# Scores and exponentials of three heads at a time, in two sets of three PSUM banks

## The chip, the cores and the metric

The kernel runs on one core of a Trainium2 chip. The metric is the device time of one execution in microseconds (us). Before the change it is 911.02 us, the median of three runs (908.71 to 912.02).

## The reference

One block of a vision-language model: gated cross attention, then a gated feed-forward part. There are 4 batches of 512 rows of x with 512 channels, 1024 context rows per batch, 16 heads of 32 channels and 1536 hidden channels. Cut to what matters:

```python
q  = qdq(layernorm(x)) @ qdq(wq).T + bq              # qdq: fake int8 rounding
k, v = split(ctx @ wkv.T + bkv)
attn = softmax(einsum("bnhd,bmhd->bhnm", q, k) / sqrt(32))
o  = einsum("bhnm,bmhd->bnhd", attn, v)
x  = x + tanh(g_xattn) * (qdq(o) @ qdq(wp).T + bp)
y  = layernorm(x)
h  = silu((y @ gate_w) * gate_scale) * ((y @ up_w) * up_scale)
x  = x + tanh(g_ffn) * ((h @ down_w) * down_scale)
```

## The kernel before

The kernel is written engine by engine: each engine has its own program, in the order of the text, and semaphores tie them together. Batches are worked one after the other. For batch b TensorE (PE) runs the attention units, then a list `D_SEQ[b]` of products: the output projection, the next batch's keys, values and queries, the feed-forward part. Beside these, the next batch's row maxima are prepared (`maxima`, `differences`), from which comes a shift that each row of scores has subtracted, so that the exponential needs no maximum of its own.

**Units.** The attention of a batch has 4 groups (g) of 4 heads, and a group has 8 tiles (t) of 128 context rows: 32 units (u = 8 g + t). One unit is, for 4 heads j:

- `scores`: four f16 matmuls (97 rows deep, 128 keys by 512 queries), each into a PSUM bank of its own. L1569.
- the exponential on ScalarE (ACT), from PSUM into `prob` in SBUF (shown as tile r). L907. Before the change it takes two banks, so two heads, in one instruction of 128x1024.
- `values`: four f32 matmuls of 32 columns, side by side in TensorE, that add prob times the values into `O_BANK`. L1586. The trace shows each f32 matmul as two passes, so a unit as x8.
- the denominators: in batches 1 to 3, VectorE (DVE) adds up `prob` of the units t = 0 to 6 of a group in `acc` (`add_unit`, L1149, two adds of 128x1024 a unit, none at t = 0, whose prob goes in with t = 1). Then TensorE multiplies `acc` with a selector into `DEN_BANK` (`totals`, L1614, x8 in the trace). The last unit of a group, t = 7, isn't added by DVE but goes to TensorE itself (`sums`, L1600).

**Order on TensorE.** For each u: scores(u), values(u - 1), sums(u - 1) where that is a t = 7, and at t = 0 of a later group totals(g - 1). So the matmuls of the next unit's scores are queued behind totals, and totals waits for the last add of its group (`p_dve`).

**Buffers.** `prob` holds 12 heads, three units: the exponential of unit u waits until unit u - 3 has been used by `values` (`p_used`) and, if it is an added one, by DVE (`p_dve`). `acc` exists once: the first add of a group waits for the totals of the group before (`acc_read`), and that first add is what frees prob of the units t = 0 and t = 1. The output of a group is copied out of `O_BANK` by ACT (L911) before the next group's first `values` may start.

**PSUM banks in batches 1 to 3.** `SCORES[1] = (0, 6, 2)`: three pairs of banks, 0-1, 6-7 and 2-3, taken in turn, so the scores of pair n wait for the exponential of pair n - 3. Bank 4 is `O_BANK`, bank 5 `DEN_BANK`. While the stage before is still running, banks 4 to 7 serve the maxima (`DIFF`, `PAIR`) and 0 to 3 the products (`FREE_RING`).

**DVE** has one more job in the units of batches 1 and 2: the next batch's x (`x_ahead`: layer norm and rounding), a piece ahead of the add of each unit in `AHEAD_UNITS`, which is (3, 8 to 24). Batch 3 has none.

**DMA.** The stacked keys and queries (`kst`, `qst`) hold two groups. SyncE loads group g = 2 and 3 once the last scores of group g - 2 are issued: 24 DMAs and one for the shift row.

Batch 0 works in another way (single heads at first, no adds on DVE) and isn't touched by the change.

Of the kernel before, what the change touches and what calls it, by code (L numbers as in the profile page):

```python
# [8 lines left out]
ACT = mybir.ActivationFunctionType  # L9
# [6 lines left out]
P = 128  # L16
B, N, C = 4, 512, 512
M = 1024
H, DH = 16, 32
F = 1536  # L20
HG = P // DH
G = H // HG
# [13 lines left out]

FREE_RING, HEAD_RING = (0, 1, 2, 3), (0, 1, 2, 3, 4, 5)
O_BANK, DEN_BANK, PAIR = 4, 5, 6  # L40
DIFF, DIFF0 = 4, 2
SCORES = ((0, 2), (0, 6, 2))
K_SEQ0 = [f"K{n}" for n in (0, 2, 4, 6, 1, 3, 5, 7)]
TURNED = ["SX"] + [f"XT{c}" for c in range(CT)]
EARLY_V = ["V0", "V1"]
# [112 lines left out]
UNITS = G * MT  # L158
# [57 lines left out]
def v_out_count(name):  # L216
    return int(name[1:]) - len(EARLY_V) + 1
# [15 lines left out]
def d_seq(b):  # L233
    return D_SEQ[b]
# [11 lines left out]
def d_bank(b, name):  # L246
    return D_BANK[b][name]
# [33 lines left out]


def single(b, u):

    return b == 0 and u < SINGLES


def score_bank(b, u, j):
    if single(b, u):
        return j % 2  # L290
    return SCORES[b > 0][(2 * (u if b else u - SINGLES) + j // 2) % len(SCORES[b > 0])]


def diff_bank(b, s):
# [4 lines left out]
    return b * len(DIFFS) + DIFFS.index(s) + 1  # L299


def exp_count(b, u, j):

    if single(b, u):
        return HG * u + j + 1
    return HG // 2 * (b * UNITS + u + SINGLES) + j // 2 + 1


LAST_BANK = D_BANK[B - 1][f"DOWN{NT - 3}"]
# [21 lines left out]
def build(nc, ctxT, x, wq, wkvT, wp, gate_w, up_w, down_w, bqT, bkT, bv, bp, gsT, usT, ds,  # L331
          g_x, g_f, out):
    with ExitStack() as ctx:
# [452 lines left out]
        def _(act):  # L786
# [84 lines left out]
            def projection_weights(u):  # L871

                if u in WP_ROWS:
                    half = WP_ROWS.index(u)
                    integer_rows(DVE_WP, range(2 * half, 2 * half + 2))
                if ("W", 0, 0) in UNIT_MIDS0.get(u, []):
                    act.wait_ge(consts_in, 5 * 16)
                    act.wait_ge(act_setup, 1)
                    nc.scalar.activation(bp_bc[:, :], bp_bc[:, :], ACT.Copy, scale=tg_c[:, 0:1]).then_inc(act_setup, 1)
                    nc.scalar.activation(ds_bc[:, :], ds_bc[:, :], ACT.Copy, scale=tg_c[:, 1:2]).then_inc(act_setup, 1)  # L880
                    act.wait_ge(pe_setup, 2)
                    for half in range(2):
# [7 lines left out]
            act.wait_ge(pool_setup, 3)  # L890

            for b in range(B):
                nc.scalar.activation(table[:, :], zero[:, :], ACT.Exp)
                for u in range(UNITS):
                    g, t = divmod(u, MT)
                    freed = u - P_RING[b > 0]
                    if freed >= 0:
                        act.wait_ge(p_used, b * UNITS + freed + 1)
                    heads = 1 if single(b, u) else 2
                    for j in range(0, HG, heads):  # L900
                        if j == 2 and b == 0 and u >= 1:
                            differences(0, UNIT_STEPS0[u - 1])
                        if freed >= 0 and added(b, freed):
                            act.wait_ge(p_dve, add_count(b, freed, j + 1))
                        s, first_bank = p_slot(b, u, j), score_bank(b, u, j)
                        act.wait_ge(s_full, exp_count(b, u, j))
                        nc.scalar.activation(prob[:, s:s + heads, :], ps[:, first_bank:first_bank + heads, :], ACT.Exp,  # L907
                                             scale=SCALE).then_inc(exp_done, 1)
                    if t == 0 and g > 0:
                        act.wait_ge(o_full, b * G + g)  # L910
                        nc.scalar.copy(oT[:, g - 1, :], bank(O_BANK)).then_inc(o_out, 1)  # L911
                    if b == 0:
                        projection_weights(u)
                act.wait_ge(p_used, (b + 1) * UNITS)
                nc.scalar.copy(denT, bank(DEN_BANK)).then_inc(den_out, 1)  # L915
# [481 lines left out]
        def _(pe):  # L1397
# [147 lines left out]
            def scores(b, u, j):  # L1545

                g, t = divmod(u, MT)
                first_bank, n, ring = score_bank(b, u, j), 2 * u + j // 2, len(SCORES[b > 0])
                if t == 0 and j == 0:
                    rows = b if g % 2 else 0  # L1550
                    pe.wait_ge(stack_in[g % 2], ((b * 2 + g // 2 + 1) * STACK_DMAS + rows) * 16)
                if single(b, u):
                    if u == 0 and j < 2:
                        pe.wait_ge(v_out, v_out_count(f"V{MT - 1}"))
                    else:
                        pe.wait_ge(exp_done, exp_count(b, u, j) - 2)
                elif n >= (ring if b else 2 * SINGLES + ring):
                    pe.wait_ge(exp_done, exp_count(b, u, j) - ring)
                elif b == 0 and first_bank == DIFF0:
                    pe.wait_ge(diff_kept, len(DIFFS))  # L1560
                elif b == 0:
                    pe.wait_ge(exp_done, exp_count(b, u - 1, HG - 1))
                elif first_bank == PAIR:
                    pe.wait_ge(m_free, FREE_AFTER[b, STREAM[-1]])
                else:
                    for k in range(2):
                        released(b - 1, [n for n in d_seq(b - 1) if d_bank(b - 1, n) == first_bank + k][-1])
                for k in range(1 if single(b, u) else 2):
                    mm = nc.tensor.matmul(bank(first_bank + k), kst[0:97, g % 2, j + k, t * P:(t + 1) * P],  # L1569
                                          qst[0:97, g % 2, j + k, :], start=True, stop=True)  # L1570
                mm.then_inc(s_full, 1)

            def values(b, u):

# [19 lines left out]
            def sums(b, u):  # L1594

                if added(b, u):
                    return
                g = u // MT
                for j in range(HG):
                    mm = nc.tensor.matmul(ps[j * DH:(j + 1) * DH, DEN_BANK, :], esel[:, g, :],  # L1600
                                          prob[:, p_slot(b, u, j), :], start=(u == (MT - 1 if b else 0)), stop=(u == UNITS - 1))
                mm.then_inc(p_used, 1)

# [6 lines left out]
            def totals(b, g):  # L1610

                pe.wait_ge(p_dve, add_count(b, g * MT + ADDED[g][-1], HG - 1))
                for j in range(HG):
                    mm = nc.tensor.matmul(ps[j * DH:(j + 1) * DH, DEN_BANK, :], esel[:, g, :], acc[:, j, :],  # L1614
                                          start=False, stop=False)
                if g < G - 1:
                    mm.then_inc(acc_read, 1)
# [55 lines left out]

            for b in range(B):
                last = b == B - 1
                for u in range(UNITS):
                    g, t = divmod(u, MT)
                    scores(b, u, 0)
                    scores(b, u, 1 if single(b, u) else 2)
                    if u >= 1:  # L1680
                        values(b, u - 1)
                    if single(b, u):
                        scores(b, u, 2)
                        scores(b, u, 3)
                    for s in UNIT_MIDS0.get(u, []) if b == 0 else []:
                        maxima(b, s)
                    if u >= 1:
                        sums(b, u - 1)
                    for s in UNIT_STEPS0[u] if b == 0 else []:
                        maxima(b, s)  # L1690
                    if b > 0 and t == 0 and g > 0:
                        totals(b, g - 1)
                values(b, UNITS - 1)
                if b > 0:
                    totals(b, G - 1)
# [122 lines left out]
```

## Time and profile before

| what | us |
|---|---|
| median of three runs | 911.02 |
| the profiled execution | 908.2 |
| its span | 906.4 |
| TensorE busy | 852.7 (94%) |
| VectorE busy | 673.0 (74%) |
| ScalarE busy | 556.6 (61%) |
| attention units of batch 1, first exponential to the denominators' copy | 326.40 to 400.29 |
| the same of batch 2 | 538.68 to 612.84 |
| the same of batch 3 | 738.62 to 809.67 |

Busy times of TensorE come from pipelined matmuls whose ends are modelled: a share of 94% says that it is nearly always occupied, not that it works at its peak. The granted clock of TensorE was 0.998 of full speed over the span. In the rows, `ps` is PSUM, `r` the tile of prob, `vv` the values, `acc` the running sums, `qst` and `kst` the stacked queries and keys.

### The profile page before, as it was taken

Reading aid. Unit: us, or ns where it says so; the run is one execution under the profiler, and the core shown is the slowest. Engines: PE = TensorE matmul, PEld = TensorE weight load, DVE = VectorE, ACT = ScalarE, POOL = GpSimd, SP = SyncE. Lnnn points to the kernel's source line nnn. Section 1 sums busy time; section 2 is a strip of 40 time slices with the busy share of each in tenths; the row PEclk is TensorE's granted clock in tenths of the full one; section 3 lists DMA queues with packets and bytes.
Section 4 is the critical chain, followed back from the end, with each engine's and each line's share of the span. In section 5 each row is a group of like instructions: output and inputs, shape, how many; then the busy total and the mean of one; then the engine's idle time right before and its main releaser. Section 6 shows DMA issues by size and latency. Waiting matters only on the chain.

```text
span 906.4 us, 13628 instructions
## 1 busy us (share of the span) xinstructions
PE 852.7 (94%) x4974; PEld 314.0 (35%) x4982; DVE 673.0 (74%) x1300; ACT 556.6 (61%) x743; POOL 252.8 (28%) x241
## 2 busy tenths in 40 slices
PE   5989999999999999999899999999999989998998
PEld 1422222244333332234433332224433322234444
DVE  6877967989766788878666778986867778788222
ACT  5557988752466569772555659874356679862330
POOL 1335766872257400020017700002002210020230
PEclk9999999999999999999999999999999999999999
DMA  9334244221211332100111143200010023200001
GB/s 329 105 97 125 84 118 116 80 83 49 50 36 47 99 106 62 44 1 1 44 33 48 38 117 101 67 1 1 15 39 1 1 63 102 53 1 24 12 0 47
DMA packets 37251, 55.29 MB, mean 61 GB/s; under 512 B 8960, under 2 KB 15424, under 8 KB 37184
## 3 DMA queue, kind: packets, MB, share of 16 engines
q1 hardware_dynamic: 35264, 48.13, 18.7%
q0 software_dynamic: 1920, 6.29, 2.3%
q8 instruction: 39, 0.64, 0.3%
q14 instruction: 28, 0.23, 0.1%
HBM read 31.21 MB, written 4.19 MB: 39 GB/s over the span
## 4 chain that ended last, share of the span: by engine, by line
PE 69%; DVE 15%; ACT 8%; issue 7%; DMA 1%; ACTq 0%; DVEq 0%
PE ps L1418 34%; PE ps L1606 9%; PE ps L1586 8%; PE ps L1569 8%; ACT r L907 5%; PE ps L1541 4%; DVE acc L1149 4%; PE ps L1600 4%; PE ps L1614 1%; DVE kst L1124 1%; DVE am L1004 1%; PE ps L1402 1%; DVE xs L1334 1%; DVE r L1290 1%; ACT r L930 1%
## 5 line engine op out<-in xcount | busy, mean ns | idle before, releaser
L907 ACT ACTIVATE r<-ps 128x1024 f32<-128x1024 f32 (+1 forms) x300 | 253.3, 902 | 53.6 <-PE ps L1569 51.1
L1124 DVE CUSTOM_DVE_ANT_0 kst<-ps,kst 128x512 f32<-128x512 f32 x192 | 124.5, 685 | 30.3 <-PE ps L1541 28.9
L1586 PE MATMUL ps<-r,vv 128*32 128x512 f32 x1024 | 137.3, 608 | 3.4 <-ACT r L907 3.2
L1569 PE MATMUL ps<-qst,kst 97*128 97x512 f16 x512 | 138.0, 384 | 2.6 <-ACT r L907 1.4
L1149 DVE TENSOR_TENSOR acc<-acc,r 128x1024 f32<-128x1024 f32 x120 | 138.6, 1215 | 0.0
L861 ACT ACTIVATE kst<-ps 128x1024 f32<-128x1024 f32 x96 | 98.1, 1022 | 54.2 <-PE ps L1474 53.9
L1418 PE MATMUL ps<-xs,w_gate 128*128 128x512 f16 x384 | 91.0, 380 | 2.0 <-DVE xs L1334 2.0
L1418 PE MATMUL ps<-xs,w_up 128*128 128x512 f16 x384 | 91.1, 380 | 0.0
L1569 PEld LDWEIGHTS ps<-qst,kst 97*128 97x128 f16 x512 | 40.5, 97 | 139.3 <-ACT r L907 88.1
L962 ACT ACTIVATE qst<-ps,gs_c 128x512 f32<-128x512 f32 x48 | 33.0, 687 | 68.0 <-PE ps L1418 68.0
L1364 DVE SCALAR_TENSOR_TENSOR xq<-ps,us_c,qst 128x512 f32<-128x512 f32 x48 | 36.0, 749 | 50.6 <-PE ps L1418 50.6
L1606 PE MATMUL ps<-w_down,r 128*128 128x512 f16 (+1 forms) x312 | 66.2, 363 | 0.0
L1418 PE MATMUL ps<-ctx_hi,wkv_hi 128*128 128x512 f16 x128 | 49.1, 389 | 14.3 <-ACT ctx_hi L797 10.9
L777 POOL TENSOR_TENSOR r<-xq,r 128x512 f16<-128x512 f32 x36 | 42.6, 1183 | 70.4 <-ACT r L955 70.0
L1474 PE MATMUL ps<-acc,q_reg 32*128 32x512 f16 x256 | 49.7, 384 | 4.7 <-issue 3.6
L1541 PE MATMUL ps<-k_reg,q_reg 32*128 32x512 f16 x256 | 49.7, 385 | 4.5 <-DVE mx L1124 3.9
L1418 PEld LDWEIGHTS ps<-xs,w_gate 128*128 128x128 f16 x384 | 35.6, 98 | 47.0 <-issue 5.2
L727 POOL TENSOR_TENSOR xres<-xres,bp_bc 128x512 f32<-128x512 f32 x12 | 14.9, 1269 | 129.7 <-ACT r L915 129.1
L1418 PEld LDWEIGHTS ps<-xs,w_up 128*128 128x128 f16 x384 | 34.6, 98 | 45.0 <-issue 8.1
L688 POOL TENSOR_TENSOR rstd<-mv,mhalf 128x4 f32<-128x4 f32 x8 | 9.9, 1240 | 141.4 <-DVE mv L1035 141.4
L1418 PE MATMUL ps<-ctx_lo,wkv_hi 128*128 128x512 f16 x128 | 48.9, 387 | 0.3 <-DVE ctx_lo L1159 0.3
L1149 DVE TENSOR_TENSOR acc<-r 128x1024 f32<-128x1024 f32 x24 | 28.3, 1222 | 27.7 <-ACT r L907 27.7
(173 smaller groups left out, 1347.9 us busy)
## 6 DMA issues: line engine op xcount, KB each, us to landing
kst<-k_reg SPq DMA_DIRECT2D x192, 64.0 KB
qst<-q_reg SPq DMA_DIRECT2D x192, 32.0 KB
xs<-in_x SPq DMA_DIRECT2D x4, 1024.0 KB, 5.9
cf<-in_ctxT POOLq DMA_DIRECT2D x16, 256.0 KB, 3.4
xres<-in_x SPq DMA_DIRECT2D x3, 1024.0 KB, 5.2
out<-xres SPq DMA_DIRECT2D x12, 256.0 KB, 2.0
acc<-in_down_w SPq DMA_DIRECT2D x10, 256.0 KB, 2.6
vv<-in_wkvT SPq DMA_DIRECT2D x2, 1024.0 KB, 9.7
```

Source lines behind the costliest of these rows:

```text
L777: nc.gpsimd.tensor_tensor(f2_at(b, 1, i), fus[:, i % 2, :], f2_at(b, 0, i), ALU.subtract).then_inc(f_ready, 1)
L861: nc.scalar.activation(kept(b, n), ps[:, first_bank:first_bank + 2, :], ACT.Relu, scale=2.0).then_inc(diff_kept, 1)
L907: nc.scalar.activation(prob[:, s:s + heads, :], ps[:, first_bank:first_bank + heads, :], ACT.Exp, scale=SCALE).then_inc(exp_done, 1)
L1124: ins = nc.vector.tensor_tensor_reduce(kept(b, n)[:, k, :], bank(PAIR + k), kept(b, n)[:, k, :], 1.0, -3.0e38, ALU.add, ALU.max, mx[:, g % ...
L1149: nc.vector.tensor_tensor(sums, other, prob[:, p:p + ADD_HEADS, :], ALU.add).then_inc(p_dve, 1)
L1418: mm = nc.tensor.matmul(out, l, r, start=(k == 0), stop=(k == len(terms) - 1))
L1474: mm = nc.tensor.matmul(bank(first_bank + k), qhi[rows, g, i // 2 * P:(i // 2 + 1) * P], kdiff[rows, g % 2, :], start=True, stop=True)
L1541: mm = nc.tensor.matmul(bank(PAIR + k), qhi[rows, g, t * P:(t + 1) * P], khi[rows, g, 512:1024], start=True, stop=True)
L1569: mm = nc.tensor.matmul(bank(first_bank + k), kst[0:97, g % 2, j + k, t * P:(t + 1) * P], qst[0:97, g % 2, j + k, :], start=True, stop=True)
L1586: mm = nc.tensor.matmul(ps[j * DH:(j + 1) * DH, O_BANK, :], vv[:, t, h * DH:(h + 1) * DH], prob[:, p_slot(b, u, j), :], start=(t == 0), st ...
L1600: mm = nc.tensor.matmul(ps[j * DH:(j + 1) * DH, DEN_BANK, :], esel[:, g, :], prob[:, p_slot(b, u, j), :], start=(u == (MT - 1 if b else 0) ...
L1606: mm = nc.tensor.matmul(out[:, cols], f2_at(b, part, i)[:, t * P:(t + 1) * P], w_down[:, i, cols], start=(i == 0 and part == 0), stop=(i = ...
```

## The change

In batches 1 to 3 the 128 heads of a batch's units are no longer handled in 64 pairs but in 43 steps of three (the last has two). A step may hold heads of two units. `THREES = (5, 0)`: steps take banks 5, 6, 7 and banks 0, 1, 2 in turn, so step n waits for the exponential of step n - 2. The denominators move from bank 5 to bank 3 in these batches. TensorE issues the scores of step n, and then values and sums of each unit whose last head lies in a step up to n - 2; totals(g - 1) now stands behind values of the next group's first unit, and no longer ahead of it.

```diff
-O_BANK, DEN_BANK, PAIR = 4, 5, 6
+O_BANK, DEN_BANK, PAIR = 4, (5, 3), 6
-SCORES = ((0, 2), (0, 6, 2))
+SCORES, THREES = (0, 2), (5, 0)
...
+def three(n):
+
+    return range(3 * n, min(3 * n + 3, UNITS * HG))
...
+STEPS_0 = HG * SINGLES + HG // 2 * (UNITS - SINGLES)
+STEPS_B = -(-UNITS * HG // 3)
...
+                for n in range(STEPS_B if b > 0 else 0):
+                    heads = three(n)
+                    freed = sorted({h // HG - P_RING[1] for h in heads})
+                    if freed[-1] >= 0:
+                        act.wait_ge(p_used, b * UNITS + freed[-1] + 1)
+                    for u in freed:
+                        if u >= 0 and added(b, u):
+                            act.wait_ge(p_dve, add_count(b, u, heads[-1] % HG if u == freed[-1] else HG - 1))
+                    s, first_bank = p_slot(b, 0, heads[0]), THREES[n % 2]
+                    act.wait_ge(s_full, exp_count(b, 0, heads[0]))
+                    nc.scalar.activation(prob[:, s:s + len(heads), :], ps[:, first_bank:first_bank + len(heads), :],
+                                         ACT.Exp, scale=SCALE).then_inc(exp_done, 1)
+                    for h in heads:
+                        g, first = divmod(h - HG + 1, MT * HG)
+                        if first == 0 and g > 0:
+                            turned_out(b, g)
...
+            def scores_of_three(b, n):
+                first_bank = THREES[n % 2]
+                for h in three(n):
+                    if h % (MT * HG) == 0:
+                        stacked(b, h // (MT * HG))
+                if n >= 2:
+                    pe.wait_ge(exp_done, STEPS_0 + (b - 1) * STEPS_B + n - 1)
+                elif first_bank == DIFF + 1:
+                    pe.wait_ge(diff_kept, (b + 1) * len(DIFFS))
+                    pe.wait_ge(m_free, FREE_AFTER[b, STREAM[-1]])
+                else:
+                    for k in range(3):
+                        products_done(b, first_bank + k)
+                for k, h in enumerate(three(n)):
+                    mm = score(b, h // HG, h % HG, first_bank + k)
+                mm.then_inc(s_full, 1)
...
-                    if b > 0 and t == 0 and g > 0:
-                        totals(b, g - 1)
+                done = UNITS - 1 if b == 0 else 0
+                for n in range(STEPS_B + 2 if b > 0 else 0):
+                    if n < STEPS_B:
+                        scores_of_three(b, n)
+                    while done < UNITS - 1 and (done * HG + HG - 1) // 3 <= n - 2:
+                        values(b, done)
+                        sums(b, done)
+                        if done % MT == 0 and done > 0:
+                            totals(b, done // MT - 1)
+                        done += 1
```

The start of batch 1's units on TensorE, before. L1606 is the last product of the stage ahead (bank 3), L1569 are scores, L1586 values:

```order
L1606 MATMUL ps<-w_down,r 128x512 x8
L1569 MATMUL ps<-qst,kst 128x512 x8
L1586 MATMUL ps<-r,vv 32x512 x4
L1569 MATMUL ps<-qst,kst 128x512 x4
L1586 MATMUL ps<-r,vv 32x512 x4
L1569 MATMUL ps<-qst,kst 128x512 x4
```

The same place after the change, where L1659 are the products, L1583 scores and L1637 values:

```order
L1659 MATMUL ps<-w_down,r 128x512 x8
L1583 MATMUL ps<-qst,kst 128x512 x12
L1637 MATMUL ps<-r,vv 32x512 x4
L1583 MATMUL ps<-qst,kst 128x512 x3
L1637 MATMUL ps<-r,vv 32x512 x4
L1583 MATMUL ps<-qst,kst 128x512 x3
L1637 MATMUL ps<-r,vv 32x512 x4
L1583 MATMUL ps<-qst,kst 128x512 x6
```

Twelve heads of scores now stand ahead of the first values, not eight. From there on, blocks of 3, 3 and 6 score matmuls alternate with values, where there were blocks of 4; the number of blocks is one for each unit either way.

The first border between groups on TensorE, from values(6) on, before. L1600 are sums, L1614 totals:

```order
L1586 MATMUL ps<-r,vv 32x512 x4
L1569 MATMUL ps<-qst,kst 128x512 x4
L1586 MATMUL ps<-r,vv 32x512 x4
L1600 MATMUL ps<-r,esel 32x512 x4
L1614 MATMUL ps<-acc,esel 32x512 x4
L1569 MATMUL ps<-qst,kst 128x512 x4
L1586 MATMUL ps<-r,vv 32x512 x4
L1569 MATMUL ps<-qst,kst 128x512 x4
```

The same after the change, with L1653 sums and L1667 totals:

```order
L1637 MATMUL ps<-r,vv 32x512 x4
L1583 MATMUL ps<-qst,kst 128x512 x3
L1637 MATMUL ps<-r,vv 32x512 x4
L1653 MATMUL ps<-r,esel 32x512 x4
L1583 MATMUL ps<-qst,kst 128x512 x3
L1637 MATMUL ps<-r,vv 32x512 x4
L1667 MATMUL ps<-acc,esel 32x512 x4
L1583 MATMUL ps<-qst,kst 128x512 x6
L1637 MATMUL ps<-r,vv 32x512 x4
L1583 MATMUL ps<-qst,kst 128x512 x3
```

Between sums and totals there are now three score matmuls and the values of unit 8. Behind totals come six score matmuls and values(9).

## Rows read from the trace of the kernel before

**Rows 1.** Windows inside batch 1's units, no border inside: us, then busy (x) of PE, PEld, DVE, ACT.
```profile
331.50:341.30 9.80, 9.80 (x64) 2.30 (x62) 9.77 (x16) 9.58 (x11) 1.89 (x1) 1.00 0.42 137
346.90:358.70 11.80, 11.80 (x76) 2.80 (x72) 11.80 (x13) 11.64 (x13) 0.00 (x0) 1.00 0.33 77
```
**Rows 2.** Chain of waits in batch 1's units: start, length, engine, tile, line.
```profile
326.40 1.95 ACT r L907 x2
...
330.52 0.99 PE ps L1586 x8
331.52 0.97 PE ps L1569 x4
...
342.31 1.00 PE ps L1586 x8
343.31 0.86 PE ps L1600 x8
344.17 0.86 PE ps L1614 x8
345.68 1.03 ACT r L907
...
396.12 1.03 ACT r L907
397.19 1.07 PE ps L1586 x8
398.29 1.07 PE ps L1614 x8
```
**Rows 3.** ScalarE in order of time: batch 1 behind its three borders, batch 3 behind one.
```profile
345.68 15.72 ACT L907 ACTIVATE r<-ps 128x1024 f32<-128x1024 f32 x16 [1.27 <-PE ps L1569]
...
364.99 15.70 ACT L907 ACTIVATE r<-ps 128x1024 f32<-128x1024 f32 x16 [3.11 <-PE ps L1569]
...
383.40 13.73 ACT L907 ACTIVATE r<-ps 128x1024 f32<-128x1024 f32 x14 [2.24 <-PE ps L1569]
...
757.90 15.70 ACT L907 ACTIVATE r<-ps 128x1024 f32<-128x1024 f32 x16 [1.27 <-PE ps L1569]
```
**Rows 4.** ScalarE's groups by shape, whole span: busy, mean ns, idle before.
```profile
L907 ACT ACTIVATE r<-ps 128x1024 f32<-128x1024 f32 x212 | 205.0, 1023 | 44.6 <-PE ps L1569 42.1
...
L907 ACT ACTIVATE r<-ps 128x512 f32<-128x512 f32 x88 | 48.3, 610 | 9.0 <-PE ps L1569 9.0
```
**Rows 5.** Order of time on TensorE, batch 1: start of the units, and values(15).
```profile
320.57 3.19 PE L1606 MATMUL ps<-w_down,r 128*128 128x512 f16 x14
...
325.77 2.32 PE L1569 MATMUL ps<-qst,kst 97*128 97x512 f16 x8
...
327.48 0.11 PEld L1569 LDWEIGHTS ps<-qst,kst 97*128 97x128 f16 x2 [0.57 <-ACT r L907]
...
328.49 1.06 PE L1586 MATMUL ps<-r,vv 128*32 128x512 f32 x8 [0.40 <-ACT r L907]
...
359.69 1.07 PE L1586 MATMUL ps<-r,vv 128*32 128x512 f32 x8
```
**Rows 6.** The same, start of batch 3's units.
```profile
736.79 0.38 PE L1606 MATMUL ps<-w_down,wkv_hi 128*128 128x512 f16 x1
738.00 1.46 PE L1569 MATMUL ps<-qst,kst 97*128 97x512 f16 x6 [0.83 <-issue]
```
**Rows 7.** Order of time on VectorE, in batch 1's second group.
```profile
346.81 1.23 DVE L1149 TENSOR_TENSOR acc<-r 128x1024 f32<-128x1024 f32 x1 [2.29 <-ACT r L907]
...
358.00 2.35 DVE L1149 TENSOR_TENSOR acc<-acc,r 128x1024 f32<-128x1024 f32 x2
```
**Rows 8.** TensorE's waits in batch 1's units: total, times, longest.
```profile
PE ps L1614 <- DVE acc L1149: 2.4, 2, 1.7
```
**Rows 9.** SyncE's queue in batch 3's units, in order of time.
```profile
770.04 7.52 SPq L555 DMA_DIRECT2D qst<-q_reg  x12
777.61 7.80 SPq L555 DMA_DIRECT2D kst<-k_reg  x12
785.45 0.63 SPq L565 DMA_DIRECT2D qst<-crow  x1
```

More of the change, by code:

```diff
@@ L285, in single, with score_bank @@
     return b == 0 and u < SINGLES
[L288 to L291, printed above, removed]
+def score_bank(u, j):
+    return j % 2 if single(0, u) else SCORES[(2 * (u - SINGLES) + j // 2) % 2]
+def three(n):
+    return range(3 * n, min(3 * n + 3, UNITS * HG))
 def diff_bank(b, s):
@@ L299, in diff_count @@
     return b * len(DIFFS) + DIFFS.index(s) + 1
+STEPS_0 = HG * SINGLES + HG // 2 * (UNITS - SINGLES)
+STEPS_B = -(-UNITS * HG // 3)
 def exp_count(b, u, j):
+    if b > 0:
+        return STEPS_0 + (b - 1) * STEPS_B + (u * HG + j) // 3 + 1
     if single(b, u):
         return HG * u + j + 1
-    return HG // 2 * (b * UNITS + u + SINGLES) + j // 2 + 1
+    return HG // 2 * (u + SINGLES) + j // 2 + 1
 LAST_BANK = D_BANK[B - 1][f"DOWN{NT - 3}"]
@@ L890, in _, with turned_out @@
             act.wait_ge(pool_setup, 3)
+            def turned_out(b, g):
+                if added(b, g * MT - 1):
+                    act.wait_ge(p_used, b * UNITS + g * MT)
+                else:
+                    act.wait_ge(o_full, b * G + g)
+                nc.scalar.copy(oT[:, g - 1, :], bank(O_BANK)).then_inc(o_out, 1)
             for b in range(B):
                 nc.scalar.activation(table[:, :], zero[:, :], ACT.Exp)
-                for u in range(UNITS):
+                for u in range(UNITS if b == 0 else 0):
                     g, t = divmod(u, MT)
-                    freed = u - P_RING[b > 0]
+                    freed = u - P_RING[0]
                     if freed >= 0:
-                        act.wait_ge(p_used, b * UNITS + freed + 1)
+                        act.wait_ge(p_used, freed + 1)
                     heads = 1 if single(b, u) else 2
                     for j in range(0, HG, heads):
-                        if j == 2 and b == 0 and u >= 1:
+                        if j == 2 and u >= 1:
                             differences(0, UNIT_STEPS0[u - 1])
-                        if freed >= 0 and added(b, freed):
-                            act.wait_ge(p_dve, add_count(b, freed, j + 1))
-                        s, first_bank = p_slot(b, u, j), score_bank(b, u, j)
+                        s, first_bank = p_slot(b, u, j), score_bank(u, j)
                         act.wait_ge(s_full, exp_count(b, u, j))
@@ L909, in _ @@
                     if t == 0 and g > 0:
[L910 to L913, printed above, removed]
+                        turned_out(b, g)
+                    projection_weights(u)
+                for n in range(STEPS_B if b > 0 else 0):
[13 more added lines that the diff above has]
+                        if first == 0 and g > 0:
+                            turned_out(b, g)
                 act.wait_ge(p_used, (b + 1) * UNITS)
-                nc.scalar.copy(denT, bank(DEN_BANK)).then_inc(den_out, 1)
+                nc.scalar.copy(denT, bank(DEN_BANK[b > 0])).then_inc(den_out, 1)
                 nc.scalar.copy(oT[:, G - 1, :], bank(O_BANK)).then_inc(o_out, 1)
@@ L1543, in maxima, with stacked, score @@
                 mm.then_inc(m_full, 1)
-            def scores(b, u, j):
+            def stacked(b, g):
+                rows = b if g % 2 else 0
+                pe.wait_ge(stack_in[g % 2], ((b * 2 + g // 2 + 1) * STACK_DMAS + rows) * 16)
+            def score(b, u, j, out):
                 g, t = divmod(u, MT)
[L1548 to L1559, printed above, removed]
-                    pe.wait_ge(diff_kept, len(DIFFS))
-                elif b == 0:
-                    pe.wait_ge(exp_done, exp_count(b, u - 1, HG - 1))
-                elif first_bank == PAIR:
@@ new lines, in score, with scores @@
+                return nc.tensor.matmul(bank(out), kst[0:97, g % 2, j, t * P:(t + 1) * P], qst[0:97, g % 2, j, :],
+                                        start=True, stop=True)
+            def scores(u, j):
+                first_bank = score_bank(u, j)
+                if u % MT == 0 and j == 0:
+                    stacked(0, u // MT)
+                if u == 0 and j < 2:
+                    pe.wait_ge(v_out, v_out_count(f"V{MT - 1}"))
+                elif single(0, u) or u > SINGLES:
+                    pe.wait_ge(exp_done, exp_count(0, u, j) - 2)
+                elif first_bank == DIFF0:
+                    pe.wait_ge(diff_kept, len(DIFFS))
+                else:
+                    pe.wait_ge(exp_done, exp_count(0, u - 1, HG - 1))
+                for k in range(1 if single(0, u) else 2):
+                    mm = score(0, u, j + k, first_bank + k)
+                mm.then_inc(s_full, 1)
@@ L1565, in scores @@
                 else:
[L1566 to L1570, printed above, removed]
+                    for k in range(3):
+                        products_done(b, first_bank + k)
@@ L1571, in scores, with products_done @@
+                for k, h in enumerate(three(n)):
+                    mm = score(b, h // HG, h % HG, first_bank + k)
                 mm.then_inc(s_full, 1)
+            def products_done(b, bank_no):
+                released(b - 1, [n for n in d_seq(b - 1) if d_bank(b - 1, n) == bank_no][-1])
             def values(b, u):
@@ L1597, in sums @@
                     return
+                if b > 0 and u == MT - 1:
+                    products_done(b, DEN_BANK[1])
                 g = u // MT
                 for j in range(HG):
-                    mm = nc.tensor.matmul(ps[j * DH:(j + 1) * DH, DEN_BANK, :], esel[:, g, :],
+                    mm = nc.tensor.matmul(ps[j * DH:(j + 1) * DH, DEN_BANK[b > 0], :], esel[:, g, :],
                                           prob[:, p_slot(b, u, j), :], start=(u == (MT - 1 if b else 0)), stop=(u == UNITS - 1))
@@ L1613, in totals @@
                 for j in range(HG):
-                    mm = nc.tensor.matmul(ps[j * DH:(j + 1) * DH, DEN_BANK, :], esel[:, g, :], acc[:, j, :],
+                    mm = nc.tensor.matmul(ps[j * DH:(j + 1) * DH, DEN_BANK[b > 0], :], esel[:, g, :], acc[:, j, :],
                                           start=False, stop=False)
@@ L1675, in _ @@
                 last = b == B - 1
[L1676 to L1679, printed above, removed]
+                for u in range(UNITS if b == 0 else 0):
+                    scores(u, 0)
+                    scores(u, 1 if single(b, u) else 2)
                     if u >= 1:
@@ L1682, in _ @@
                     if single(b, u):
-                        scores(b, u, 2)
-                        scores(b, u, 3)
-                    for s in UNIT_MIDS0.get(u, []) if b == 0 else []:
+                        scores(u, 2)
+                        scores(u, 3)
+                    for s in UNIT_MIDS0.get(u, []):
                         maxima(b, s)
@@ L1688, in _ @@
                         sums(b, u - 1)
-                    for s in UNIT_STEPS0[u] if b == 0 else []:
+                    for s in UNIT_STEPS0[u]:
                         maxima(b, s)
-                    if b > 0 and t == 0 and g > 0:
-                        totals(b, g - 1)
+                done = UNITS - 1 if b == 0 else 0
[8 more added lines that the diff above has]
+                        done += 1
+                assert done == UNITS - 1
                 values(b, UNITS - 1)
```

## The prediction, made blind

> **What bounds the units now.** I read first the windows of each stage, then the chain of waits inside the attention units, then ScalarE and VectorE in order of time there, and last the waits by engine. Only the units of batches 1 to 3 change, some 70 us each, so nothing outside them is priced.
>
> Within a group TensorE is busy 9.80 of 9.80 us and 11.80 of 11.80 [rows 1]. ScalarE looks full too (11.64 of 11.80), but its rows carry the write-back, which overlaps with the next instruction: two exponentials take 1.95 us and one 1.03, so a new one can start every 0.92 us, 1.84 us a unit [rows 2]. Sixteen of them, eight units, in fact took 15.72 us, 1.96 us a unit [rows 3]. That is TensorE's pace: the chain goes through nothing but scores (0.97) and values (0.99), 1.96 us [rows 2]. ScalarE has about 0.12 us of slack a unit.
>
> At a border between groups 0.86 for sums and 0.86 for totals come in, and ScalarE then idles 1.27 us behind its copy of the output [rows 2, 3]. This is TensorE's work, and stays. Behind the second and third border of batch 1 it idles 3.11 and 2.24 us instead [rows 3]: 1.84 + 0.97 = 2.8 us more, because totals waits for VectorE's last add (2.4 us in two waits [rows 8]). Batch 2 has these two again, batch 3, without next x on VectorE, none.
>
> **Exponentials of three.** 64 instructions a batch become 43. From 610 ns for 512 columns and 1023 for 1024 [rows 4] I take 413 to 430 ns a bank, so 1.45 us for 1536, and a new one every 0.92 + 0.43 = 1.35 us. This is the unknown operation; its bounds are 1.38 (two banks and a quarter less for the third) and 1.63 (the two rows added). ScalarE's need falls from 1.84 to 1.80 us a unit. TensorE's stays: four score matmuls, one block of values and two changes of kind a unit, 1.96 us. So the steady stretch gains nothing. It may lose a little: with two sets of banks, where two steps of scores stand together, the second needs an exponential that has just ended. A score matmul takes (3.19 - 0.38)/13 = 0.216 us [rows 5, 6], so a block of three takes 0.97 - 0.22 = 0.75 with the change of kind, 0.65 without. If a step's scores start at 0, its exponential starts at 0.85 and ends at 2.30; the scores two steps on are due at 0.75 + 0.99 + 0.65 = 2.39. That is nearly free: 0 to 0.05 us for each such pair, 0.2 us a batch.
>
> The Trainium skill (Perfetto Trace Analysis, "Optimizing Scalar/DVE Operations") says that larger ScalarE operations raise throughput if that engine is saturated, with some 51 ns of overhead for each one on PSUM. By the rule, an estimate, the 21 instructions saved would give 1.1 us a batch. The same section says that where ScalarE is not saturated but causes gaps on others, smaller instructions can be better; the trace puts this kernel on that side.
>
> **The start, per batch +0.9.** Before, from the first score matmul to values(0) it is 328.49 - 325.77 = 2.72 us, 8 score matmuls inside [rows 5]. After: first exponential at 0.85 (0.63 now and a third matmul), end 2.30, scores of step 2 at 2.36 (0.06 after an exponential's end, as at 327.48 [rows 2, 5]); second exponential at 0.85 + 1.35 = 2.20, end 3.65, scores of step 3 at 3.71, values(0) at 4.46. Four more matmuls are inside, 0.86 us of work done early. Loss: 4.46 - 2.72 - 0.86 = 0.9.
>
> In batch 3 the first scores wait 0.83 us and more for bank 0, which VectorE still empties [rows 6]. After, step 0 takes banks 5 to 7 and can follow the last product at 736.79 + 0.22: 1.0 us earlier. So -1.0 in batch 3. In batches 1 and 2 bank 3 held the last product, and its wait is already in the 2.72.
>
> **The borders: the ring of prob behind late totals.** This is the step I put most weight on. acc is single: totals(g - 1), then the first add of group g, then prob of that group's unit 0 is free, then the exponential three units on may start. Totals now stands one unit later, but the ring is still three units. For the first border, from the start of totals: totals 1.07 [rows 2], 0.10 to VectorE (an exponential ended at 346.71, the add began at 346.81 [rows 2, 7]), the first half of the add 1.23 [rows 7], 0.10 to ScalarE, the exponential of step 14 1.45, 0.05 to TensorE: scores of step 16 at 4.00. TensorE's own work until there: totals with change of kind 0.99, six score matmuls with a change 1.40, values 0.99: 3.38. It idles 0.6. At the second border the same count comes out, 0.6. At the third the step that needs the ring holds three heads of one unit, so both halves of the add are needed (+1.13): 5.1 against 0.99 + 0.75 + 0.99 + 0.75 + 0.99 = 4.5, a wait of 0.65, and the next step follows without values between (0.65 against ScalarE's 1.35): 0.7 more. Sum of a batch: 0.6 + 0.6 + 1.35 = 2.6 us. In batch 3 this is all new.
>
> In batches 1 and 2 totals no longer waits for the add, -2.8 us. But VectorE paces the second group: its adds and pieces of x follow one another without a gap. Its first add starts later than now. From the start of values(7) the order gives values 0.89, sums 0.97, scores 0.75, values(8) 0.89, totals 1.07 and 0.10, so 4.67; now it is 346.81 - 342.31 = 4.50 [rows 2, 7]. And values(7) itself comes 1.6 us later, 0.9 from the start and 0.65 for three heads more that are issued ahead of it. So +1.75. The half of unit 13's add that the exponential of head 64 needs ends at 358.00 + 1.22 now, then at 360.97; exponential from 361.07 to 362.52, scores of step 23 at 362.6. TensorE is at this point of its work, where values(15) is the next block of values, at 359.69 now [rows 5]; with one score matmul more (0.2) and the 1.55 lost so far (0.9, 0.6 and a steady pair) it is there at 361.45. Wait 1.1. Behind it I expect smaller ones of this kind, 0.7 together (bounds 0 and 1.5). So the wait on VectorE isn't removed but moves from totals into the ring. Borders of batch 1: 2.6 + 1.1 + 0.7 - 2.8 = +1.6, and batch 2 alike.
>
> **The end of the units.** Before, TensorE waits 0.76 us for the last exponential and 0.2 for the last add (397.19 after values(30), 398.29 [rows 2]). After, the last step has two heads and starts sooner, but the last add then decides: 0.9 in sum. 0, bounds -0.4 and +0.5. The denominators in bank 3: 0, since that bank's last product is long out at unit 7.
>
> **Sum.** Batch 1: 0.9 + 0.2 + 1.6 = 2.7; batch 2: 2.7; batch 3: 0.9 + 0.2 + 2.6 - 1.0 = 2.7. Together +8.1 on the profiled 908.2, so 916.3. The median is 2.8 above the profiled run, so 919.0 us. No change can be told below 0.5%, 4.6 us.
>
> **Rivals.**
> - *No stall from the ring.* If VectorE's first add of a group starts soon enough, or the exponentials run further behind than I count, the 2.6 us a batch and the 1.1 + 0.7 fall away. Batches 1 and 2: 0.9 + 0.2 - 2.8 = -1.7 each, batch 3 +0.1: 907.7 us. For it: VectorE idles 2.29 us at the first border now [rows 7]. Against: that gap ends with an exponential behind totals, and the order puts totals still later. A case between, with half the stalls, is 913.5.
> - *ScalarE is what paces.* Then what it saves counts: 64 x 0.92 - 43 x 1.35 = 0.8 us a batch, or 21 x 0.16 = 3.4 if an instruction's whole fixed part falls away (610 less 430 to 450 ns for the columns), besides the 2.8 of two batches: 911 - 5.6 - 2.4 to 10.2, so 895 to 903. Against: 1.96 is TensorE's sum to the hundredth. By the skill's 51 ns this would be 3.2 us over three batches beside the 5.6.
> - *Slower still, by the keys' DMA.* Group 3's loads take 785.45 + 0.63 - 770.04 = 16.0 us to issue, from the last scores of group 1 [rows 9]. TensorE needs them 8 units of 1.96 and a border of 1.7 and a little later, 18.1 now. After the change a step reaches over a group's border and values are issued further behind, so the need comes at 17.4. If the last load takes over 1.4 us to land, each of up to 6 borders waits up to 1 us: 922 to 925.
> - *A dearer exponential.* At 1.55 us the start, the borders and the steady pairs each grow by one or two tenths: +2.3 in all, 921.3. At 1.63, 923.
>
> **Chances.** My sum with small deviations (916 to 921) 0.55; with the DMA or a dearer exponential (above 921) 0.17; half the stalls (911 to 916) 0.13; no stall 0.09; ScalarE as the pace 0.06. Range 911.5 to 923.5, which leaves the last two and the far end out. Faster by over 0.5% (below 906.5) 0.06, within 0.5% 0.18, slower by over 0.5% (above 915.6) 0.76.
>
> **What would show it.** Right: in the changed profile each exponential of 128x1536 near 1.45 us; inside groups TensorE still 1.96 us a unit; no wait of totals on VectorE before the last; instead scores waiting for exponentials behind each border, and ScalarE idle there until an add ends; values(0) some 4.5 us behind the first score matmul, where it is 2.7 now. Wrong: exponentials that start without a wait for an add three units back; ScalarE without gaps and units of 1.80 us; or a wait on stack DMAs of a microsecond at the borders.

## The result and the profile after

| | median us | against the kernel before |
|---|---|---|
| before | 910.5 (6 runs) | |
| after | 918.2 (916.3 to 920.0, 6 runs) | ratio 1.008, 95% interval 1.0061 to 1.0098 |

The change makes the kernel slower, by 7.7 us. The forecast was 919.0, between 911.5 and 923.5. The profiled execution of after has a span of 914.4 us, 8.0 more than before.

The page of after shows first what the change was able to do. Section 1, busy time and instructions of each engine:

```profile
PE 856.9 (94%) x4982; PEld 312.2 (34%) x4982; DVE 673.7 (74%) x1300; ACT 550.8 (60%) x680; POOL 253.1 (28%) x241
```

ScalarE has 63 instructions fewer and 5.8 us less busy time. Its exponentials of three, in the stretch of batch 1's units, by shape (out and in, count, busy us, mean ns, idle before and what ended it; batch 1's last step, of two heads, isn't among them):

```profile
L939 ACT ACTIVATE r<-ps 128x1536 f32<-128x1536 f32 x42 | 59.1, 1454 | 17.5 <-PE ps L1583 10.7 <-DVE acc L1180 6.4
```

1454 ns is the 1.45 us of the prediction. Before, all the idle time ahead of batch 1's exponentials was ended by score matmuls. Now 6.4 us of it is ended by an add of VectorE.

The start of batch 1's units on TensorE, in order of time, answers to [rows 5]:

```profile
326.08 1.46 PE L1583 MATMUL ps<-qst,kst 97*128 97x512 f16 x6
328.43 0.82 PE L1583 MATMUL ps<-qst,kst 97*128 97x512 f16 x3 [0.90 <-ACT r L939]
329.77 0.82 PE L1583 MATMUL ps<-qst,kst 97*128 97x512 f16 x3 [0.52 <-ACT r L939]
330.52 1.07 PE L1637 MATMUL ps<-r,vv 128*32 128x512 f32 x8
```

Values(0) starts 4.44 us after the first score matmul; it was 2.72. The third and fourth steps each wait for an exponential.

The chain of waits in batch 1 answers to [rows 2], first inside the first group, then from values(7) over the border:

```profile
337.54 0.75 PE ps L1583 x3
338.29 0.99 PE ps L1637 x8
339.29 0.76 PE ps L1583 x3
340.04 0.99 PE ps L1637 x8
341.04 1.45 PE ps L1583 x6
342.49 0.99 PE ps L1637 x8
...
344.24 0.99 PE ps L1637 x8
345.24 0.86 PE ps L1653 x8
346.10 0.75 PE ps L1583 x3
346.85 1.00 PE ps L1637 x8
347.85 0.90 PE ps L1667 x8
348.77 1.28 DVE acc L1180 x2
```

Three units now take 0.75 + 0.99 + 0.76 + 0.99 + 1.45 + 0.99 = 5.93 us of TensorE; before they took 3 x 1.96 = 5.88. A third head in one instruction bought nothing in the steady stretch, as it is TensorE's. What is new is that the chain leaves TensorE behind totals and goes on through VectorE. The same border in order of time, all engines:

```profile
348.77 2.36 DVE L1180 TENSOR_TENSOR acc<-r 128x1024 f32<-128x1024 f32 x2 [3.47 <-PE ps L1667]
...
350.08 4.14 ACT L939 ACTIVATE r<-ps 128x1536 f32<-128x1536 f32 x3 [1.49 <-DVE acc L1180]
...
351.59 0.82 PE L1583 MATMUL ps<-qst,kst 97*128 97x512 f16 x3 [0.49 <-ACT r L939]
```

VectorE is idle for 3.47 us until totals has read `acc`, ScalarE for 1.49 us until the first add has freed prob, TensorE for 0.49 until that exponential is done. In [rows 7] VectorE's idle time at this place was 2.29 us and ended by an exponential.

For the whole stretch, from the start of the last product ahead of the units to the copy of the denominators (us, from the rows of each profile; before in batch 1: 325.55 to 400.29):

| profile | batch 1 | batch 2 | batch 3 | sum | against before |
|---|---|---|---|---|---|
| before | 74.7 | 75.0 | 72.9 | 222.6 | |
| after | 77.2 | 77.2 | 76.0 | 230.4 | +7.7 |
| threes_totals_early | 76.6 | 75.0 | 74.7 | 226.2 | +3.6 |
| threes_early_pool_keys | 75.0 | 75.0 | 73.6 | 223.5 | +0.9 |
| pairs_totals_late | 72.3 | 72.3 | 73.4 | 218.0 | -4.6 |
| pairs_late_bank6 | 72.3 | 72.3 | 72.2 | 216.8 | -5.8 |
| pairs_late_two_sets | 75.6 | 75.6 | 75.7 | 226.9 | +4.2 |
| pairs_short_exp | 74.2 | 74.5 | 72.7 | 221.4 | -1.2 |

The 7.7 us of the change are these stretches; all that lies outside them is 0.3 us longer than before.

### The profile page after: what moved, and what is told of

It reads as the page before. It is cut to its first block, busy times and chain, and to the rows that moved or that the text cites. A ratio compares the mean times of both kernels' runs of the same rounds, so it can differ in the third digit from the quotient of the medians.

```text
span 914.4 us, 13570 instructions
## 1 busy us (share of the span) xinstructions
PE 856.9 (94%) x4982; PEld 312.2 (34%) x4982; DVE 673.7 (74%) x1300; ACT 550.8 (60%) x680; POOL 253.1 (28%) x241
## 4 chain that ended last, share of the span: by engine, by line
PE 67%; DVE 16%; ACT 8%; issue 7%; SPq 2%; DMA 1%; ACTq 0%; DVEq 0%
PE ps L1449 33%; PE ps L1659 9%; PE ps L1583 7%; PE ps L1637 7%; DVE acc L1180 5%; PE ps L1572 4%; ACT r L939 4%; PE ps L1653 4%; SPq L566 2%; PE ps L1667 1%; DVE kst L1155 1%; ACT r L924 1%; PE ps L1433 1%; DVE am L1035 1%; DVE xs L1365 1%
## 5 line engine op out<-in xcount | busy, mean ns | idle before, releaser
L939 ACT ACTIVATE r<-ps 128x1536 f32<-128x1536 f32 (+1 forms) x129 | 180.0, 1444 | 47.4 <-PE ps L1583 29.2
L1583 PE MATMUL ps<-qst,kst 97*128 97x512 f16 x512 | 141.0, 385 | 14.7 <-ACT r L939 12.4
L1637 PE MATMUL ps<-r,vv 128*32 128x512 f32 x1024 | 137.2, 608 | 0.6
L872 ACT ACTIVATE kst<-ps 128x1024 f32<-128x1024 f32 x96 | 98.2, 1023 | 54.2 <-PE ps L1505 53.9
L1583 PEld LDWEIGHTS ps<-qst,kst 97*128 97x128 f16 x512 | 38.5, 97 | 156.8 <-ACT r L939 75.6
L924 ACT ACTIVATE r<-ps 128x512 f32<-128x512 f32 (+1 forms) x108 | 67.7, 686 | 18.3 <-PE ps L1583 18.3
L1659 PE MATMUL ps<-w_down,r 128*128 128x512 f16 (+1 forms) x312 | 66.2, 363 | 0.0
```

What stands on the lines that cost most here:

```text
L872: nc.scalar.activation(kept(b, n), ps[:, first_bank:first_bank + 2, :], ACT.Relu, scale=2.0).then_inc(diff_kept, 1)
L939: nc.scalar.activation(prob[:, s:s + len(heads), :], ps[:, first_bank:first_bank + len(heads), :], ACT.Exp, scale=SCALE).then_inc(exp_done, 1)
L1583: return nc.tensor.matmul(bank(out), kst[0:97, g % 2, j, t * P:(t + 1) * P], qst[0:97, g % 2, j, :], start=True, stop=True)
L1637: mm = nc.tensor.matmul(ps[j * DH:(j + 1) * DH, O_BANK, :], vv[:, t, h * DH:(h + 1) * DH], prob[:, p_slot(b, u, j), :], start=(t == 0), st ...
L1659: mm = nc.tensor.matmul(out[:, cols], f2_at(b, part, i)[:, t * P:(t + 1) * P], w_down[:, i, cols], start=(i == 0 and part == 0), stop=(i = ...
```

## Experiments

Each run was timed beside fresh executions of the kernel before, and its ratio is against those: their median was 910.9 us for the first four runs below, and 911.2 for the last two. The clock of TensorE isn't the same in all executions, and two medians can differ by it; the last section and the account ahead of it say by how much.

**threes_totals_early** takes the late totals out of the changed kernel and leaves the steps of three:

```diff
-                        if done % MT == 0 and done > 0:
-                            totals(b, done // MT - 1)
+                        if done % MT == MT - 1:
+                            totals(b, done // MT)
```

> The changed kernel, but totals of a group stand right behind sums of its last unit, ahead of the next score matmuls, as in the kernel before. Theory (late totals hold the ring of prob: first add late, so the exponential three units on late): the waits of scores behind the borders (0.5 at the first, up to 1.4 with ScalarE behind it) go at the first and third border; the wait of totals on VectorE comes back in part in batches 1 and 2 (about 0.5 us at the third border). About 2.1 us less in each of the three batches, so 918.2 - 6.4 = 911.8 us, near the kernel before (within 0.3%). Rival (the loss comes from the three-head steps themselves, totals' place is harmless or useful): at least as slow as the changed kernel, 918 to 922 us, since VectorE's waits of 2.8 us in two batches come back.

Measured: 914.2 us (12 runs), ratio 1.0032 (1.0017 to 1.0047) against 1.008. So late totals costs 4.0 us by the medians of the two kernels, and the rival, that it is harmless, falls. ScalarE at the same border, in order of time:

```profile
347.22 1.46 ACT L939 ACTIVATE r<-ps 128x1536 f32<-128x1536 f32 x1
349.26 1.45 ACT L939 ACTIVATE r<-ps 128x1536 f32<-128x1536 f32 x1 [0.58 <-PE ps L1583]
351.01 1.45 ACT L939 ACTIVATE r<-ps 128x1536 f32<-128x1536 f32 x1 [0.30 <-PE ps L1583]
```

No exponential waits for an add there now. But the time is 2.4 us above what I expected. By stretches: batch 1 has a spell at a lower granted clock (last section), 1.6 us of this profile; without it, batches 1 and 2 lie 0.3 and 0.0 above the kernel before, as expected, and batch 3 lies 1.8 above, where 2.1 us less than the changed kernel would be 1.1. TensorE waits for the shift row's DMA, the last load of a group, longer than in the changed kernel. Batch 2 has two such waits and batch 3 one of 0.5 us; the last line is a second one of batch 3, seen from the weight load, while the matmul's own row puts its 0.82 us on an exponential:

```profile
573.39 0.82 PE L1583 MATMUL ps<-qst,kst 97*128 97x512 f16 x3 [0.60 <-DMA qst<-crow]
...
592.09 0.82 PE L1583 MATMUL ps<-qst,kst 97*128 97x512 f16 x3 [0.47 <-DMA qst<-crow]
...
772.53 0.33 PEld L1583 LDWEIGHTS ps<-qst,kst 97*128 97x128 f16 x3 [1.72 <-DMA qst<-crow]
```

**pairs_totals_late** is the other corner: the kernel before, with late totals only.

```diff
-                    if b > 0 and t == 0 and g > 0:
+                    if b > 0 and t == 1 and g > 0:
                         totals(b, g - 1)
```

> The kernel before with its pairs and three sets of two banks, but totals of a group one unit later. Theory (the ring has room for late totals as long as pairs are issued less far ahead, and VectorE's wait at the borders was the only recoverable loss): TensorE's waits for VectorE in batches 1 and 2 nearly vanish, 2.3 us each, batch 3 loses 0.3 us at most: 910.5 - 4.3 = 906.2 us. Rival (late totals stall the ring here as they do with threes): the 2.8 us saved at the borders come back as waits of scores for exponentials, and batch 3 loses 1 to 2 us: 910.5 to 913 us.

Measured: 906.6 us (8 runs), ratio 0.9943 (0.9922 to 0.9965). Against the 910.9 beside it, the same move that costs 4 us with the threes gains 4.3 with the pairs. TensorE's waits in batch 1's units, where [rows 8] had 2.4 us on VectorE:

```profile
PE ps L1614 <- DVE acc L1149: 0.3, 1, 0.3
```

ScalarE in order of time shows why the ring doesn't stall it:

```profile
361.92 0.58 ACT L911 COPY k_reg<-ps 128x512 f32<-128x512 f32 x1
362.77 2.11 ACT L907 ACTIVATE r<-ps 128x1024 f32<-128x1024 f32 x2 [0.28 <-DVE acc L1149]
365.58 9.82 ACT L907 ACTIVATE r<-ps 128x1024 f32<-128x1024 f32 x10 [0.70 <-PE ps L1569]
```

Once it is held for 0.28 us by an add, in a place where it has that slack. The stretches of batches 1 and 2 fall from 74.7 and 75.0 to 72.3 us, by 2.4 and 2.7 where 2.3 each was expected. Batch 3 grows from 72.9 to 73.4, by 0.6 where at most 0.3 was expected; a score matmul there waits 0.2 us for the shift row's DMA.

**pairs_late_bank6** also changes the order of the pairs' sets: `SCORES = ((0, 2), (6, 0, 2))`, where the last entry was (0, 6, 2).

> As the one before, with the pairs' sets in the order 6, 0, 2 instead of 0, 6, 2: the first pair of a batch no longer takes the bank that the last product still holds in batch 3. Theory: first scores of batch 3 start 0.9 to 1.0 us earlier (before 1.2 us behind the last product's last matmul), nothing changes in batches 1 and 2: 905.2 us. Rival (the start there waits for the maxima or the keys' DMA): no difference from the one before, 906.2 us.

Measured: 904.9 us (6 runs), ratio 0.9931 (0.9906 to 0.9955); this is the lowest median of all. The times don't separate it from the one before, the trace does: batch 3's stretch is 72.2 and not 73.4. Its start answers to [rows 6]:

```profile
733.02 0.38 PE L1606 MATMUL ps<-w_down,wkv_hi 128*128 128x512 f16 x1
733.24 0.60 PE L1569 MATMUL ps<-qst,kst 97*128 97x512 f16 x2
734.19 1.47 PE L1569 MATMUL ps<-qst,kst 97*128 97x512 f16 x6 [0.35 <-DVE acc L1224]
```

The first scores follow the product after 0.22 us, where there were 1.21.

**pairs_short_exp** asks whether ScalarE paces the units. It leaves work out: in batches 1 to 3 an exponential covers 448 of 512 columns.

```diff
-                        nc.scalar.activation(prob[:, s:s + heads, :], ps[:, first_bank:first_bank + heads, :], ACT.Exp,
-                                             scale=SCALE).then_inc(exp_done, 1)
+                        cols = N if b == 0 else N - 64
+                        nc.scalar.activation(prob[:, s:s + heads, 0:cols], ps[:, first_bank:first_bank + heads, 0:cols],
+                                             ACT.Exp, scale=SCALE).then_inc(exp_done, 1)
```

> The kernel before, but in batches 1 to 3 each exponential covers 448 of the 512 columns of its two heads (the others keep what prob held), so each is about 0.11 us shorter. Theory (TensorE paces the units, ScalarE has slack): units stay at 1.96 us; only starts and ends of a batch gain, 0.3 to 0.5 us each: 909.3 us, within the noise. Rival (ScalarE paces, and saving there would count): 64 x 0.11 = 6.8 us a batch, about 890 us.

Measured: 910.3 us (10 runs), ratio 0.9993 (0.9978 to 1.0008). Each exponential fell from 1023 to 916 ns, and its start to start could too, but in order of time two of them are followed by a gap, every 1.96 us:

```profile
336.23 1.73 ACT L908 ACTIVATE r<-ps 128x896 f32<-128x896 f32 x2 [0.24 <-PE ps L1570]
338.19 1.73 ACT L908 ACTIVATE r<-ps 128x896 f32<-128x896 f32 x2 [0.24 <-PE ps L1570]
340.16 1.73 ACT L908 ACTIVATE r<-ps 128x896 f32<-128x896 f32 x2 [0.24 <-PE ps L1570]
```

The rival, about 890 us, falls: the units keep TensorE's period. What is taken off ScalarE turns into ScalarE's idle time, so what only makes the exponentials cheaper is worth 0.2 to 0.5 us a batch here, at the ends.

**pairs_late_two_sets** takes a set away from the pairs: `SCORES = ((0, 2), (6, 0))`, all else as in pairs_totals_late.

> As pairs_totals_late, but with two sets of two banks (6-7 and 0-1) instead of three, so the scores of pair n wait for the exponential of pair n - 2. Theory (two sets are part of the price of the threes: TensorE can no longer run ahead of ScalarE over its values block): scores wait for exponentials inside groups too, values(0) comes later, about 3.2 us more in each batch than pairs_totals_late, less the 1.0 us that batch 3 gains at its start: 906.5 + 8.6 = 915.1 us. Rival (a third set is never needed in the steady stretch, only late totals cost): 905.5 to 907.5 us.

Measured: 914.3 us (10 runs), ratio 1.0038 (1.0022 to 1.0054). So 7.7 us for the third set; the stretches say 8.9, and I had expected 8.6. In order of time ScalarE now loses 0.27 us after every fourth exponential, inside the group:

```profile
334.72 3.99 ACT L907 ACTIVATE r<-ps 128x1024 f32<-128x1024 f32 x4 [0.40 <-PE ps L1569]
338.97 3.98 ACT L907 ACTIVATE r<-ps 128x1024 f32<-128x1024 f32 x4 [0.27 <-PE ps L1569]
```

So the third set is what the pairs live on. The ring of prob isn't what it guards: with two sets of pairs TensorE's waits in batch 1 are 1.0 and 0.4 us, at the start and at the end, and none stands behind a border. That points to the steps of three and their order of issue for the stall behind late totals, and not to the missing set alone; it isn't proof, as two units of pairs take 4.25 us here and not 3.92, which gives the ring some time. The changed kernel has late totals and two sets too, and its stretches take 230.4 us where this one's take 226.9: with late totals, steps of three heads don't repay the third set, they add 3.5 us to its loss. Whether they would with early totals wasn't tried.

**threes_early_pool_keys** takes threes_totals_early and lets GpSimd issue the key loads of groups 2 and 3, beside SyncE's loads of the queries and with semaphores of their own (TensorE's waits for them are left out here):

```diff
-                    stack(kst, (khi, khi, klo), g, upto[3:])
                     if b == 0:
+                        stack(kst, (khi, khi, klo), g, upto[3:])
...
+                    for g in range(2, G):
+                        pool.wait_ge(s_full, exp_count(b, (g - 1) * MT - 1, HG - 1))
+                        for dst4, src in enumerate((khi, khi, klo)):
+                            for j in range(HG):
+                                pool.dma_start(kst[dst4 * DH:(dst4 + 1) * DH, g % 2, j, :],
+                                               src[j * DH:(j + 1) * DH, g, :]).then_inc(keys_in[g % 2], 16)
```

> As threes_totals_early, but in batches 1 to 3 the twelve key DMAs of groups 2 and 3 are issued by GpSimd, beside SyncE's twelve of the queries, so that the last load of a group is issued some 7 us sooner. Theory (the 1.1 us that threes_totals_early lies above its expectation is score matmuls that wait for the last of a group's DMAs): the waits on the shift row's DMA (1.1 us in batch 2, 0.5 in batch 3) vanish: about 1.6 us less, 912.6 us. Rival (GpSimd's descriptors slow VectorE's adds, or the keys come later still from that queue): waits on VectorE or on the keys grow, 914 to 920 us.

Measured: 914.4 us (10 runs), ratio 1.0023 (1.0009 to 1.0037), where 912.6 us was expected. The interval overlaps that of threes_totals_early, so the time alone is inconclusive. In the trace the waits on the DMA are gone in all three batches. Batch 3 gains 1.1 us, and its 0.82 us of above is gone too, so that was the DMA. Batch 2 gains nothing: there VectorE's adds and its pieces of x pace the units. The 1.1 us of DMA wait in batch 2 are replaced: TensorE's waits on ScalarE grow from 1.7 to 2.6 us and those on VectorE from 0.5 to 0.7, 3.3 in sum with either kernel:

```profile
PE ps L1593 <- ACT r L946: 2.6, 4, 0.9
PE ps L1677 <- DVE acc L1187: 0.7, 2, 0.5
```

## Why the prediction was right, point by point

- *TensorE bounds the units.* Shown: after the change the chain keeps to TensorE inside batch 1's first group, and shorter exponentials change nothing in the kernel before. In the second group of batch 1 the chain runs through VectorE's adds, as the prediction had it.
- *An exponential of three banks takes 1.45 us and a new one starts every 1.35.* 1454 ns measured, and two in a row take 2.80 us, so 1.35 from start to start. Right.
- *Steady stretch 0 to 0.05 us a pair of steps that stand together.* 5.93 against 5.88 us for three units. Right.
- *Start: values(0) at 4.46.* 4.44. The loss of 0.9 us a batch stands. The removed third set is its cause only in part: pairs_late_two_sets, with eight heads ahead of it as before, has values(0) at 3.2, 0.5 later than before.
- *Batch 3 starts 1.0 us earlier.* Its first scores follow the last product in 0.22 us, before 1.21. Right.
- *The ring behind late totals.* Right at all three borders; the links (totals to VectorE, first half of the add, exponential, scores) stand in the rows in that order, and taking totals back removes the stalls. The idle time in a row counts from the modelled end of the matmul ahead, and the prediction counted from the time at which the block was due, so the two can't be set side by side. Counted in the prediction's way: at the first border values start at 350.03 and take 1.00, so scores were due at 351.03 and start at 351.59, 0.56 late, against 0.6. At the second it is 0.55 against 0.6, at the third 0.59 and 0.69 against 0.65 and 0.7. That is 2.4 us in a batch, against 2.6. The second and the third border of batch 1:

```profile
371.27 0.82 PE L1583 MATMUL ps<-qst,kst 97*128 97x512 f16 x3 [0.38 <-ACT r L939]
...
391.21 0.82 PE L1583 MATMUL ps<-qst,kst 97*128 97x512 f16 x3 [0.52 <-ACT r L939]
392.55 0.82 PE L1583 MATMUL ps<-qst,kst 97*128 97x512 f16 x3 [0.52 <-ACT r L939]
```

- *VectorE's pace in group 1.* I put 1.1 us on the scores of step 23 at 362.6. They start at 362.85; they were due 0.65 behind 361.04, so 1.16 late. Behind it I had 0.7 in smaller waits, and scores are 0.26 late at 365.72, 0.42 at 379.39 and 0.12 at 384.5, 0.8 together:

```profile
362.85 0.82 PE L1583 MATMUL ps<-qst,kst 97*128 97x512 f16 x3 [0.99 <-ACT r L939]
...
365.72 0.82 PE L1583 MATMUL ps<-qst,kst 97*128 97x512 f16 x3 [0.19 <-ACT r L939]
```

- *End of the units: 0.* Counted in the same way, the blocks at the end of batch 1 are 0.16, 0.20 and 0.54 late, 0.9 together, where they were 0.85 and 0.22, 1.1 together: -0.2, within the bounds. As predicted, the last add now decides.
- *Sum.* I had 2.7 us for each batch. Measured are 2.4, 2.1 and 3.2 in the stretches, 7.7 against 8.1. The terms of batch 1 as measured are start 0.86, ring 2.39, VectorE 1.16 and 0.80, less 2.79 of totals' waits (1.84 and 0.95 late before) and less 0.2 at the end: 2.2, which leaves 0.2 for the steady stretches, as I had it. That the total comes within 0.4 us is in part luck, as the batches miss to both sides. The third is larger because of a rival that I had given a small chance, the keys' DMA: in batch 3 the weight load of the first score step of group 2 waits for the last DMA of the group (the idle time of the weight queue, of which 0.84 stands before any such block):

```profile
775.52 0.33 PEld L1583 LDWEIGHTS ps<-qst,kst 97*128 97x128 f16 x3 [1.29 <-DMA qst<-crow]
794.18 0.34 PEld L1583 LDWEIGHTS ps<-qst,kst 97*128 97x128 f16 x3 [1.18 <-DMA qst<-crow]
```

  That is 0.45 us. The second line, for group 3, names the DMA too, but it isn't its cause: in threes_early_pool_keys the same weight load has the same 1.18 us before it (at 790.12) while the keys are in early, and the matmul's row names an exponential. So 0.4 us at this place is a wait for ScalarE that I didn't have in the sum of batch 3 (batch 1 has it too, as the 0.42 above); why that exponential is late stays open. Batch 2 has a DMA wait of 0.55 us at 574.60 too, 1.8 us after the issue of the last load at 572.81, where the rival asked for over 1.4. It costs nothing there: the scores that wait for VectorE behind it are 0.54 us late instead of batch 1's 1.16. So this rival was no alternative but a part, of 0.45 us where I had up to 1 at each of six borders.

The account of the 7.7 us, as far as runs carry it: late totals cost 4.0 by the medians, and 5.7 by the stretches with the spell at the lower clock taken out. The clock accounts for most of the gap between the two: no execution of threes_totals_early reached the 0.996 that half of the executions of after had. At 0.994, after took 918.9 (one execution) and threes_totals_early 913.6 (mean of six), 5.3 apart, so the stretches are the better guide. The rest, 2.0 by the stretches, is the steps of three with two sets; of it, batch 3's keys that come late are 1.1 (threes_early_pool_keys; with late totals it is 0.45). What late totals could have gained is what pairs_totals_late shows, 4.3 us by the medians and 4.6 by the stretches. How the remaining 0.9 of threes_early_pool_keys over before splits between start and steady stretch wasn't tried by a run of its own; from the rows it is 0.9 a batch for the start, less batch 3's earlier start and what VectorE's shorter waits give.

## What to carry to other kernels

When an engine looks full, add up what it and its neighbour each need for the same unit, from start to start, before making its instructions fewer: here ScalarE was busy 11.64 of 11.80 us and yet needed only 1.84 us of TensorE's 1.96. A change that takes buffers away (two sets for three) and holds others longer (totals, and with it the first add and prob) has to be counted around the whole loop of who frees what for whom; a move that cost 4 us or more in one order of issue gained over 4 in another. The two parts of an edit are best tried apart: one of them alone gained 4.3 us.

## What the runs showed of the hardware that I had not expected

TensorE's granted clock falls to its lower level for short stretches, and not in the same places in each execution. In windows of 10 us, all eight profiles are at 0.90 or less between 70 and 80 us; four of them fall again, one to three times, somewhere at 200 to 240, 330 to 340 or 830 to 860 us, and the other four, before and after among them, don't. In the profile of threes_totals_early it does so right at the start of batch 1's units, behind the start's waits (TensorE busy 0.88 us of the 1.40 ahead of it). Windows there: length, busy of PE, PEld, DVE, ACT and POOL, then the granted clock, the DMA share and GB/s:

```profile
329.00:330.40 1.40, 0.88 (x8) 0.24 (x8) 0.71 (x1) 1.40 (x2) 0.00 (x0) 1.00 0.39 94
330.40:333.80 3.40, 3.40 (x16) 0.60 (x19) 3.26 (x4) 1.98 (x3) 0.00 (x0) 0.53 0.40 121
```

A granted clock of 0.53 over that window means 1.2 of 2.4 GHz for nearly all of it. In the chain values(0) takes 1.72 us there and not 1.00, the next scores 1.39 and not 0.75, the next values 1.22: 1.6 us in all. The profile of after has the same waits at the same place, and its clock stayed at 1.00, so the waits alone don't decide it. The mean clock of an execution goes with its time: beside the first four runs, the kernel before took 909.6 to 911.0 us in its executions at 0.996 and 915.1 and 915.4 at 0.988 and 0.989; after took 916.3 to 917.5 at 0.996 and 919.8 and 920.0 at 0.993. At 0.996 alone the difference of the means is 7.0 us. Differences of 2 us between medians of ten runs can be this, which is why the stretches of the profiles are set beside the times here.
